# Folding the key norms of a gated delta-rule recurrence into its scalars and values, and issuing the first expert gather earlier

## The reference

```python
# layer 1: gated delta rule with 16 heads of 16, then an MLP
k = k / (norm(k, axis=-1) + 1e-6)             # per head
def step(S, q_t, k_t, v_t, b_t, g_t):         # 512 steps, one after the other
    S = S * g_t
    kS = einsum('bhk,bhkv->bhv', k_t, S)
    S = S + b_t * einsum('bhk,bhv->bhkv', k_t, v_t - kS)
    return S, einsum('bhk,bhkv->bhv', q_t, S)
x = x + out @ Wo + bo
h = layernorm(x); x = x + gelu(h @ w1 + b1) @ w2 + b2
# layer 2: mixture of 64 experts, top 8, at most 128 rows each, and a shared expert
y[e] = (silu(xb[e] @ w_gate[e]) * (xb[e] @ w_up[e])) @ w_down[e]
out = segment_sum(y[slot] * weight, token) + shared(x)
```

## Time and profile before

| | |
|---|---|
| median of 3 executions | 2006.46 us (2003.91 to 2008.81) |
| the profiled execution | 2006.25 us, of which the span of the profile is 2004.5 us |
| mean granted TensorE clock | 0.821 |
| busy DVE, POOL, PE, ACT | 88%, 81%, 72%, 42% of the span |

### The profile page before, as it was taken

The page is one execution under the profiler, slowest core; times in us unless marked ns, Lnnn a source line. Parts: engine busy times, 40 slices in busy tenths (PEclk is TensorE's granted clock), DMA queues, the critical chain, the costliest instruction groups (busy, mean ns, idle before and its releaser), DMA issues. The chain is left out here.

```text
span 2004.5 us, 31312 instructions
## 1 busy us (share of the span) xinstructions
PE 1440.1 (72%) x8866; PEld 1250.5 (62%) x8866; DVE 1773.8 (88%) x5041; ACT 845.9 (42%) x2337; POOL 1631.7 (81%) x1367
## 2 busy tenths in 40 slices
PE   6676777887732676655655638989898988979738
PEld 5575666776622665554544627777787877858636
DVE  2689999999987999999997878999999989998980
ACT  4444455555531433333332326545554444424313
POOL 5469999898986778787878788988898999897861
PEclk9877778887765887777776859989899999979868
DMA  8664345532364647755557531233223211211110
GB/s 184 149 149 108 71 93 142 129 86 63 87 152 104 141 102 177 177 137 126 120 130 203 121 66 56 64 106 95 64 60 100 84 50 53 65 46 43 49 47 17
DMA packets 337168, 201.24 MB, mean 100 GB/s; under 512 B 208226, under 2 KB 327716, under 8 KB 336996
## 3 DMA queue, kind: packets, MB, share of 16 engines
q1 hardware_dynamic: 318724, 168.43, 34.4%
q0 software_dynamic: 15616, 30.55, 6.9%
q10 hardware_dynamic: 2656, 0.26, 0.1%
HBM read 127.58 MB, written 71.60 MB: 99 GB/s over the span
## 5 line engine op out<-in xcount | busy, mean ns | idle before, releaser
L822 POOL TENSOR_TENSOR rp<-S,qs 128x2048 f32<-128x2048 f32 x113 | 513.7, 4546 | 102.5 <-DVE S L1130 78.4
L1115 DVE SCALAR_TENSOR_TENSOR vwin<-S,gwin,bank 128x256 f32<-128x256 f32 x1024 | 482.9, 472 | 0.3
L1130 DVE SCALAR_TENSOR_TENSOR S<-S,gwin,bank 128x256 f32<-128x256 f32 x1024 | 481.8, 471 | 0.3
L1120 DVE TENSOR_REDUCE nu<-vwin 128x16 f32<-128x272 f32 x1024 | 436.7, 427 | 0.3
L1124 DVE TENSOR_TENSOR bank<-nu,bank 128x256 f32<-128x256 f32 x1024 | 429.4, 419 | 0.6
L1754 PE MATMUL bank<-region 128*128 128x128 f32 x2048 | 290.3, 302 | 0.0
L1754 PEld LDWEIGHTS bank<-region 128*128 128x128 f32 x2048 | 274.9, 216 | 18.7 <-issue 18.3
L830 POOL TENSOR_TENSOR r<-rp 128x1024 f32<-128x1024 f32 x113 | 274.7, 2431 | 7.1
L1633 PE MATMUL bank<-xaT,wqkvg 128*128 128x128 f32 (+1 forms) x1792 | 241.8, 288 | 11.3 <-ACT xaT L1323 8.2
L1765 PE MATMUL bank<-region 128*128 128x256 f32 x1024 | 234.2, 383 | 0.0
L1633 PEld LDWEIGHTS bank<-xaT,wqkvg 128*128 128x128 f32 (+1 forms) x1792 | 216.3, 190 | 25.4 <-ACT xaT L1323 11.8
(11 more groups left out here) (158 smaller groups left out, 2401.5 us busy)
## 6 DMA issues: line engine op xcount, KB each, us to landing
qkv_d<-stg SPq DMA_DIRECT2D x192, 128.0 KB, 2.3
region<-in_L_ffn_w_gate SPq DMA_DIRECT2D x64, 192.0 KB
region<-in_L_ffn_w_up SPq DMA_DIRECT2D x64, 192.0 KB
region<-in_L_ffn_w_down SPq DMA_DIRECT2D x64, 192.0 KB
region<-in_L_attn_x SPq DMA_DIRECT2D x16, 512.0 KB, 7.4
region<-in_L_attn_x SPq DMA_DIRECT2D x32, 256.0 KB, 4.8
xw_d<-region SPq DMA_DIRECT2D x32, 256.0 KB, 3.7
acc_d<-region SPq DMA_DIRECT2D x32, 256.0 KB, 4.3
```

What stands on the lines that cost most here:

```text
L822: g.tensor_tensor(rp[:, :, :].rearrange("p (a v) d -> p a v d", v=DH), S[h][:, lo:lo + HS].rearrange("p t s (v d) -> p (t s) v d", v=DH), ...
L1115: m[G] = mark(v.scalar_tensor_tensor(products_of(I, s, G)[0], earlier(h, s, G).rearrange("p (v d) -> p v d", v=DH), gwin[:, I // NB2 & 1, ...
L1120: m[G] = mark(v.tensor_reduce(nu[:, G], products_of(I, s, G)[1], AX.X, ALU.add))
L1130: ins = v.scalar_tensor_tensor(S[h][:, s, G], earlier(h, s, G), gwin[:, I // NB2 & 1, G, 1, t:t + 1], outer[G], ALU.mult, ALU.subtract)
```

## The change

The keys stay raw. For every block but the first, POOL no longer multiplies the keys by the reciprocals `r` of their norms; instead beta is multiplied by `r` (`value_factors`), the values by that product, and the scalar becomes beta times `r` squared times the gate (`scale_gates`). Both `scale_values` move to j = 6 and 7. DVE's reciprocal moves from behind step 0 to behind step 5 of j = 5. The first gather moves ahead of the second half's reads of I = 18. The six operations of `count_up` move from steps 3, 4, 5 to 4, 5, 6 from I = 19 on. ACT's last `route_exp` moves behind two copies, and PE's wait for routing constants moves from ahead of I = 0 into I = 1.

```diff
--- before.py
+++ after.py
@@ -149,9 +149,9 @@
     if I == R1 + 1:
         return {3: (0, (0, 1)), 4: (0, (2, 3)), 5: (0, (4, 5)), 6: (1, (0, 1)), 7: (1, (2, 3, 4, 5))}.get(s)
     t = I - R1
-    if I <= R1 or t >= NR or s not in (3, 4, 5):
+    if I <= R1 or t >= NR or s not in (4, 5, 6):
         return None
-    return t, (2 * s - 6, 2 * s - 5)
+    return t, (2 * s - 8, 2 * s - 7)
 
 
 ROUNDS_END = R1 + NR - 1
@@ -499,7 +499,8 @@
                 sp.wait_ge(act_staged, k * NB2)
                 sp.wait_ge(rec_done, k * NB2 * 2 + 2)
                 sp.wait_ge(*window_in(k, s))
-                sp.wait_ge(keys_ready, (k + 1) * 2)
+                if k == 0:
+                    sp.wait_ge(keys_ready, 2)
                 sp.wait_ge(vals_ready, (k + 1) * 3)
                 for i in range(BUF):
                     sp.wait_ge(f_stored[i], (min((k + 1) * NB2 + s, NT - NB2) + 1 - i) // 2 * FST)
@@ -793,11 +794,13 @@
                     n //= 2
                 g.tensor_tensor(n2[:, s, :], sq[:, 0:n], sq[:, n:2 * n], ALU.add).then_inc(n2_ready, 1)
 
-            def scale_keys(k, s):
+            def value_factors(k):
 
                 pool.wait_ge(rk_ready, k + 1)
-                kw = win[1][:, k & 1, s]
-                g.tensor_tensor(kw, kw, rk[:, s, :].unsqueeze(1).to_broadcast([P, DH, BLK]), ALU.mult).then_inc(keys_ready, 1)
+                for s in range(2):
+                    pool.wait_ge(*window_in(k, s))
+                bw = gwin[:, k & 1, :, 0]
+                link(g.tensor_tensor(bw, bw, rk[:, :, :], ALU.mult))
 
             def scale_values(k, s):
 
@@ -809,8 +812,11 @@
             def scale_gates(k):
 
                 pool.wait_ge(vals_ready, k * 3 + 2)
-                bgw = gwin[:, k & 1, :, 0]
-                g.tensor_tensor(bgw, bgw, gwin[:, k & 1, :, 1], ALU.mult).then_inc(vals_ready, 1)
+                bgw, gw = gwin[:, k & 1, :, 0], gwin[:, k & 1, :, 1]
+                if k:
+                    link(g.tensor_tensor(rk[:, :, :], rk[:, :, :], gw, ALU.mult))
+                    gw = rk[:, :, :]
+                g.tensor_tensor(bgw, bgw, gw, ALU.mult).then_inc(vals_ready, 1)
 
             def reads(I, h, half, j, mid_work=None):
 
@@ -924,19 +930,17 @@
                 back_roots(I, 0)
                 if k < NBLK and j in (3, 4):
                     square_sums(k, j - 3)
-                if k < NBLK and j == 5:
+                if k < NBLK and j == 6:
+                    value_factors(k)
                     scale_values(k, 0)
-                if k < NBLK and j in (6, 7):
-                    scale_keys(k, j - 6)
                 if k < NBLK and j == 7:
+                    scale_values(k, 1)
                     scale_gates(k)
                 if X0 <= I < X1:
                     if I + 1 < X1:
                         gather(n + 1, (n + 1) % 2)
                     reads(I, h, 0, j, lambda: scatter(n * RT, 0, h))
                     scatter(n * RT + 1, 1, h)
-                    if k < NBLK and j == 2:
-                        scale_values(k, 1)
                     if summed(I):
                         products(I, h)
                         scatter(n * RT + 2, 2, h)
@@ -948,19 +952,17 @@
                     if 1 <= i <= NRT:
                         route_weights(i - 1)
                     back_roots(I, 1)
-                    if k < NBLK and j == 2:
-                        scale_values(k, 1)
-                    if I + 1 < NI:
-                        reads(I, h, 1, j)
-                    if 1 <= I <= 1 + LATE:
-                        front_factors(I + 3)
-                        route_factors(I + 3)
                     if I == X0 - 1:
                         for i in range(BUF):
                             pool.wait_ge(r_stored[i], 64 * NB2)
                             pool.wait_ge(w_stored[i], 32 * NB2)
                         pool.wait_ge(zero_st, 32)
                         gather(0, 0)
+                    if I + 1 < NI:
+                        reads(I, h, 1, j)
+                    if 1 <= I <= 1 + LATE:
+                        front_factors(I + 3)
+                        route_factors(I + 3)
                 if h == 1:
                     relink()
                 if I == NI - 1:
@@ -1039,7 +1041,7 @@
 
             def key_factors(k):
                 dve.wait_ge(nrm_ready, k + 1)
-                dve.wait_ge(keys_ready, k * 2)
+                dve.wait_ge(vals_ready, k * 3)
                 v.reciprocal(rk[:, :, :], n2[:, :, :]).then_inc(rk_ready, 1)
 
             def stage_keys(L, G):
@@ -1234,7 +1236,7 @@
                 dve.wait_ge(prod_done, I * 2)
                 for s in range(ST):
                     step(I, h, s, at, m_)
-                    if s == 0 and j == 5 and I // NB2 + 1 < NBLK:
+                    if s == 5 and j == 5 and I // NB2 + 1 < NBLK:
                         key_factors(I // NB2 + 1)
                     r = {2: 0, 3: 1, 5: 2, 6: 3}.get(s)
                     if r is not None and (R0 <= I < R1 or X0 <= I < X1):
@@ -1262,8 +1264,11 @@
                         back_x1(i)
 
             for k in range(NBLK):
-                dve.wait_ge(keys_ready, (k + 1) * 2)
+                if k == 0:
+                    dve.wait_ge(keys_ready, 2)
                 dve.wait_ge(vals_ready, (k + 1) * 3)
+                for s in range(2):
+                    dve.wait_ge(*keys_in(k, s))
                 for s in range(2):
                     dve.wait_ge(*window_in(k, s))
                 at = {"S": [None, (rec_done, k * NB2 * 2 + 2)], "key": [stage_keys(k * NB2, G) for G in range(2)]}
@@ -1575,9 +1580,9 @@
                     front_qk(f, h)
                     front_vg(f, h)
                 if I == R1:
-                    route_exp(NRT - 1)
                     route_counts(NRT - 1, 0)
                     route_counts(NRT - 1, 1)
+                    route_exp(NRT - 1)
                 if I + 1 < NI:
                     stage(I + 1, 1 - h)
 
@@ -1686,7 +1691,6 @@
                 front_T(f, f % 2, FRONT0[f % 2][0], 1)
                 front_mm(f - 1, 1 - f % 2, FRONT0[1 - f % 2], 1)
             front_mm(AHEAD * NB2 - 1, 1, FRONT0[1], 1)
-            pe.wait_ge(const_ld, 16 * 4)
 
             def route_T(h, q, r):
                 pe.wait_ge(xn_ready, q + 1)
@@ -1797,6 +1801,8 @@
                 last.then_inc(mlp_bias, 1)
 
             def route_iteration(hf, I, h, q, f):
+                if I == 0:
+                    pe.wait_ge(const_ld, 16 * 4)
                 route_T(h, q, 0)
                 route_gu(I, q, 0)
                 route_T(h, q + 1, 1)
```

## The result

| | before | after |
|---|---|---|
| median of 4 executions each | 2007.45 us (2003.91 to 2008.81) | 1988.45 us (1987.33 to 1989.31) |
| span of the first profile | 2004.5 us | 1987.6 us |
| span of a second profile, taken with the experiments | 2008.4 us | 1982.9 us |
| mean granted TensorE clock, first profile | 0.821 | 0.823 |

The ratio of after to before is 0.9908, 95% interval 0.9891 to 0.9925: by the ratio 18.5 us faster (15.1 to 21.9). The forecast was 22 us, from 2006.25 to 1984.

A forecast was written before the change was run, and what follows sets the result against it. POOL's own sequence was taken to set the time from about I = 25 to the last scatter. Gains of 15.3 us there grew to 21.6 through the row tiles; plus 0.4, 22 us from 2006.25 gave 1984 us, range 1974 to 1995.

The forecast's parts named there:

- Part 1: Gather of I = 18 issued 15.0 us earlier: DVE gains 11.9 us, POOL's next reads start 8.1 us earlier.
- Rival (a): DVE's gain is kept because PE and ACT follow DVE, not POOL: 44 us, 1962 us; chance 0.06.
- Part 2 up to the last scatter: Key scaling removed from POOL in the expert stage, counted in full: 1.1 + 3.6 + 2.5 us.
- The I = 21 saving: Less scaling work for POOL at I = 21: 2.5 us, counted in full.
- Part 2 in the blocks behind the experts: POOL's scalings in the row tiles: 2.5 - 1.4 us around I = 37, and likewise in blocks 6 and 7.
- Part 3: Later reciprocal touches 20.8 us of DVE waits; counted 1.8 us in I = 37, 1.2 in I = 53, 0.4 elsewhere.
- The routing stage: POOL's saving worth nothing there, since POOL waits for DVE; 0.4 us taken from the reciprocal's waits.
- Part 4: PE's wait for constants moved behind I = 0 and ACT's exponential behind two copies: 0 us.
- Rival (b): POOL's saving swallowed by scatter waits, or PE late next in row tiles: 12 us, 1994; 2 to 13 us has 0.17.
- Rival (c): Scalings crowded into j = 6 and 7 start blocks late: at 5 us a block, 2019 us; chance 0.03.
- Rival (e): Gathers of I = 18 slower beside a working DVE, three times 5.1 us: 12 us gain, 1994; chance 0.02.
- the rule weighed against part 1: GpSimd can't write DMA descriptors while DVE holds the shared port pair; four gathers could cost some 16 us.

The follow-up runs named there:

- the folding alone: Changed kernel with gather, reciprocal, counting and the two small moves undone, leaving key norms folded into scalars and values: 2001.86 us, ratio 0.9965 to the kernel before.
- The last kernel of the section above: Changed kernel with POOL's output-store wait moved later, plus ACT's next front_norm ahead of an iteration's last back_norm in the row tiles: 1967.02 us, ratio 0.9791 to before.

## Why the prediction was right, and where it was not

- **Part 1, the gather: right.** DVE's 10 us wait is gone, PE's first transpose starts 0.7 us behind DVE's I = 19 where the prediction's 629.6 stood 0.1 behind it, and of DVE's 12 us only POOL's 8 last: 8.0 and 7.9 us at POOL's reads of I = 19 for 8.1 forecast. Rival (a), that DVE's gain is kept, is out; the added work in the expert stage, which came back nearly in full, shows the reason.
- **Part 2 up to the last scatter: mostly right.** The small operations cost no more than was assumed: the two took 0.62 and 0.45 us as means, for 0.7 each with its link. The I = 21 saving arrived at once in both pairs of profiles (2.3 us from POOL's reads of I = 20 to those of I = 21), but not with the folding alone (33.3 us there, 33.0 before). Over the rest of the stretch 4.9 us by the mean of all profiles, 2.5 by the two pairs of this case, for 4.7 forecast.
- **Part 2 in the blocks behind the experts: the failed step.** Here the prediction took operations on the chain of work that ended last and counted their net duration, 1.1 us in each of blocks 6 and 7, with 2.9 us for I = 35 to 37 and 1.2 for I = 53. From DVE's I = 38 to the end it took 753.8, 754.1, 753.8 and 754.4 us in the four profiles without folding and late reciprocal, 753.6 with the folding alone, 753.0 with the reciprocal alone, 753.3 and 753.7 in the changed kernel. Neither edit shortens it by more than 1 us. What stood in the way is shown by what helps: with the store wait moved it is 749.9 us from the kernel before and 746.6 from the changed one, and with `front_norm` first 739.0. An operation on the chain was not worth its duration there. At block 7 the trace shows what took the place of the gain: I = 53 is 5.8 us shorter in the first pair of profiles (32.9 to 27.1), and I = 57 and 58 are 3.3 and 1.0 us longer (24.5 to 27.8, 26.7 to 27.7), behind the store wait that grew by 3.2 us. With that wait moved I = 57 takes 24.5 us again. At block 6, where the store wait did not grow (2.99 us before, 2.22 after), the reason stays open. So does this: with the store wait moved and the reciprocal early the folded kernel takes 753.7 us from I = 38 on, the one without folding 749.9, so the folding alone gains nothing there even without the store wait. The scalings of a block then stand behind a late reciprocal, which may be the cause; it wasn't tried.
- **Part 3, the reciprocal: right in size, 2.4 us alone for 3.0 with part of the 0.4, but placed wrongly.** The 8.78 us of the earlier trace rows turned into 8.37 us for PE in the same iteration:

```profile
1223.75 0.42 DVE L1100 TENSOR_TENSOR region<-bank,region 128x256 f32<-128x256 f32 x1 [8.37 <-PE bank L1769]
```

  and the 1.8 us taken there didn't come. The 5.9 us of I = 53 did come, in whole: DVE's lead in the first pair of profiles rose from 15.7 to 21.5 us at I = 54. It was back to 16.9 by I = 59, part of it in this wait:

```profile
1750.47 0.42 DVE L1100 TENSOR_TENSOR region<-bank,region 128x256 f32<-128x256 f32 x1 [3.15 <-PE bank L1769]
```

- **The routing stage: 0.4 forecast, 6.6 measured.** "It is worth nothing there" was wrong. 2.1 us of it come in I = 2 (32.8 us before, 30.7 after) by a mechanism that is told below. Some 1.8 us come in I = 18, which takes 35.6 to 35.9 us in the profiles of the folding alone and of the changed kernel, and 37.4 to 37.7 in the six without the folding. This is the clock of TensorE and not POOL's work. DVE waits there for a matmul of PE's, 2.15 us before and 0.52 after, and PE's matmuls ahead of it take 421 ns each in the kernel before, and 275 ns from the seventh on in the changed one. The six us from 12 us behind the start of I = 18, before and then after (the last three numbers are granted clock, DMA share, GB/s):

```profile
604.10:610.10 6.00, 5.12 (x31) 4.06 (x29) 3.99 (x9) 1.45 (x7) 0.00 (x0) 0.51 0.54 126
```

```profile
600.90:606.90 6.00, 3.68 (x32) 2.94 (x30) 5.44 (x11) 2.65 (x8) 0.00 (x0) 0.82 0.58 138
```

  Before, TensorE is at the lower of its two levels (1.2 GHz) almost throughout; after, it is at the upper one (2.4 GHz) for most of it. In both PE had done nothing for 18 us or more up to 8 us behind the start of I = 18, and was at work from then on. The last kernel of the section above (ACT's norm first) has the folding as well and shows 421 ns and 37.3 us in I = 18, so the folding by itself does not bring it. The added work of I = 8 to 15, which cost 6.6 us for 20.4, says that some of POOL's time counts in this stage too. How the rest divides wasn't tried.
- **Part 4, at nothing: not contradicted.** The kernel with the counting a step later holds these two edits as well, and is 1.2 us slower, between 1.2 faster and 3.8 slower.
- **Rival (b)** named the right kind of loss, "in the row tiles PE may be late next", and a loss at the scatters that isn't borne out. **Rival (c)**, late block starts, did not come: DVE waited 5.59 us at the start of block 4 (4.11 before), but nothing there in the second profile of the changed kernel, where the second one of before had 3.0. **Rival (e)** and the rule weighed against part 1 are out: the gathers beside a working DVE took 1.09 and 0.97 us, and all 64 a mean of 972 ns, for 975 in the earlier trace rows.
- **The range** was put down with a slip: from 1974 to 1995 it takes in all of the forecast's gains of 13 to 32 us (1974 to 1993), and of rival (b)'s 2 to 13 us only the upper 2, not most.

## What to carry to other kernels

In the expert stage work added to POOL cost nearly its duration, and most likely work taken off gave it. So one kernel with some operations added in a stage is a cheap thing to try before anything is rebuilt; that it would have warned of the row tiles, where the forecast failed, is not shown, since nothing was added there. Where the change buys nothing, list that engine's waits before and after; the one that grew (here for a store's landing, which stood ahead of an instruction that doesn't write the buffer) is the next edit, and it was worth 13 us where the change itself brought 18. And a stretch with DMAs that wait for each other varies by some us from one execution to the next, so a term of that size needs several profiles on each side.

## What the runs showed of the hardware that was not expected

A DVE copy of 128 x 8 elements took 2.27 us. DVE and POOL of the kernel before, I = 2:

```profile
165.92 2.27 DVE L1029 COPY var<-region 128x8 f32<-128x8 f32 x1
...
165.82 2.34 POOL L806 TENSOR_TENSOR vwin<-vwin,gwin 128x1024 f32<-128x1024 f32 x1
```

and DVE after, where POOL has nothing to do at that time:

```profile
166.19 0.17 DVE L1031 COPY var<-region 128x8 f32<-128x8 f32 x1
```

The copy ended 25 ns behind POOL's operation. It took 2.27 to 2.29 us in all six profiles of kernels with the old scaling of the values at j = 2, and 0.17 us in all eight of kernels without it. A second such copy, in I = 4, takes 1.16 to 1.23 us beside one of POOL's sums of 1.27 us in every kernel. That agrees with the Trainium skill, SBUF — State Buffer, section "SBUF: two separate sides", by which GpSimd and a DVE operation of some kinds exclude each other for a whole instruction; of which kind this copy was, no run shows. The rule was weighed in the prediction for the DMAs of POOL, where no row shows it; it was DVE that stood still. DVE's recurrence, beside POOL's reads all the time, shows nothing of the kind: its four operations have means of 419 to 472 ns in both kernels, and none of them took over 0.54 us. Each of the three with two large inputs reads one of them from PSUM.
